# Halving the slot of the first expert layer: 23 slots of 256 rows become 39 slots of 128 rows

## What is computed

```
logits = x2 @ router_w
probs = softmax(logits); top_p, top_e = top_k(probs, 2)
for e in range(8):                                  # on the rows routed to e
    h = gelu(xd @ w_in[e] + b_in[e])                # 256 -> 256
    y = h @ w_out[e] + b_out[e]                     # 256 -> 256
out[token] += y * top_p
```

## Time and profile before

| what | value |
|---|---|
| runs | 763.7, 765.05 and 768.45 us, median 765.05 |
| profiled execution | 768.91 us, its span 767.2 us |
| mean granted clock of PE in it | 0.871 of full speed |
| busy share of the span | PE 75%, DVE 74%, POOL 57%, ACT 49% |
| the stage of the first mixture | about 303.8 to 410 us of the span |

### The profile page before, as it was taken

The page is one execution under the profiler, slowest core; times in us unless marked ns, Lnnn a source line. Parts: engine busy times, 40 slices in busy tenths (PEclk is TensorE's granted clock), DMA queues, the critical chain, the costliest instruction groups (busy, mean ns, idle before and its releaser), DMA issues.

```text
span 767.2 us, 17859 instructions
## 1 busy us (share of the span) xinstructions
PE 573.0 (75%) x6556; PEld 516.7 (67%) x6556; DVE 567.7 (74%) x1058; ACT 374.3 (49%) x567; POOL 434.3 (57%) x382
## 2 busy tenths in 40 slices
PE   5847889999999640698781556307999999999960
PEld 4636889889888530586671344206999999999950
DVE  3973579999998658587663677696777777778747
ACT  1754348777776540798560566622434343434320
POOL 7574468888898513764404885344455555555330
PEclk9988589999999885799987676657999999999995
DMA  8301001211221241699554232201011111112118
GB/s 280 99 4 29 28 2 36 71 51 55 70 68 41 73 142 54 191 309 278 151 169 144 82 99 75 80 3 56 31 55 44 56 44 54 46 51 49 36 56 309
DMA packets 35157, 68.50 MB, mean 89 GB/s; under 512 B 5761, under 2 KB 21890, under 8 KB 34818
## 3 DMA queue, kind: packets, MB, share of 16 engines
q1 hardware_dynamic: 25442, 42.70, 17.4%
q0 software_dynamic: 7488, 20.46, 9.4%
q10 hardware_dynamic: 2144, 4.19, 1.5%
HBM read 49.90 MB, written 17.43 MB: 88 GB/s over the span
## 4 chain that ended last, share of the span: by engine, by line
PE 46%; DVE 25%; issue 8%; ACT 7%; DMA 6%; POOL 6%; DVEq 1%; SPq 0%; ACTq 0%; POOLq 0%
PE banks L1249 43%; DMA sorted_y<-slot_region 2%; POOL wb_region L586 2%; PE banks L1448 2%; DVE x_res L1175 1%; DVE w_region L920 1%; DVE heads L912 1%; DVE w_region L925 1%; ACT w_region L692 1%; DMA w_region<-token_y 1%; DVE slot_region L1130 1%; DMA slot_region<-normed_rows,index 1%; DVE w_region L1060 1%; ACT w_region L625 1%; DVE slot_region L1060 1%
## 5 line engine op out<-in xcount | busy, mean ns | idle before, releaser
L1249 PE MATMUL banks<-w_region 128*128 128x128 f16 (+5 forms) x1948 | 175.7, 252 | 31.9 <-POOL w_region L548 12.1
L1249 PEld LDWEIGHTS banks<-w_region 128*128 128x128 f16 (+1 forms) x1948 | 161.0, 126 | 42.0 <-POOL w_region L548 12.4
L1249 PE MATMUL banks<-w_region,wb_region 128*128 (+1 forms) x1000 | 121.8, 278 | 11.3 <-DMA wb_region<-wk 6.7
L557 POOL DMA_INDIRECT slot_region<-normed_rows,index x85 | 94.8, 1115 | 51.0 <-PE banks L1448 21.7
L595 POOL DMA_INDIRECT token_y<-slot_region,lg x39 | 65.6, 1681 | 101.5 <-DVE slot_region L1130 101.2
L1249 PEld LDWEIGHTS banks<-w_region,wb_region 128*128 128x128 f16 (+1 forms) x1000 | 101.1, 106 | 22.9 <-issue 7.8
L759 ACT ACTIVATE wb_region<-wb_region 128x1024 f32<-128x1024 f32 x39 | 41.3, 1058 | 148.5 <-DVE wb_region L1115 148.5
L1249 PE MATMUL banks<-slot_region,staging 128*128 128x128 f16 x1872 | 112.9, 221 | 0.7 <-DVE staging L1106 0.7
L1249 PEld LDWEIGHTS banks<-slot_region,staging 128*128 128x128 f16 x1872 | 108.1, 99 | 1.0 <-issue 0.9
L1106 DVE COPY staging<-w_region 128x2048 f16 x78 | 54.5, 701 | 46.1 <-PE banks L1249 45.6
L1249 PE MATMUL banks<-wb_region,w_region 128*128 (+1 forms) x344 | 55.0, 311 | 23.2 <-DVE slot_region L1130 13.0
(11 more groups left out here) (237 smaller groups left out, 1126.1 us busy)
## 6 DMA issues: line engine op xcount, KB each, us to landing
staging<-w_t SPq DMA_DIRECT2D x24, 512.0 KB, 4.3
sorted_y<-slot_region SPq DMA_DIRECT2D x23, 256.0 KB, 5.6
w_region<-w_t SPq DMA_DIRECT2D x8, 512.0 KB, 5.5
x_res<-x SPq DMA_DIRECT2D x4, 512.0 KB, 9.4
staging<-w_in SPq DMA_DIRECT2D x4, 512.0 KB, 3.5
normed_rows<-w_region SPq DMA_DIRECT2D x16, 128.0 KB, 1.7
staging<-w_out SPq DMA_DIRECT2D x4, 512.0 KB, 3.7
normed_rows<-wb_region SPq DMA_DIRECT2D x16, 128.0 KB
```

The costliest lines, as they stand in the source:

```text
L557: g.indirect_dma_start(out=m.rows[:, j % m.RING, a, :], out_offset=None, in_=rows_dram, in_offset=bass.IndirectOffsetOnAxis(ap=index[:, q: ...
L1249: return t.matmul(o, a, b, start=start, stop=stop)
```

## The change

The first mixture gets slots of one tile as well: 39 slots of 128 rows. The ring of gathered rows holds 8 slots of 128 rows (before 3 of 256) and runs 5 slots ahead (before 2). The ring of outputs holds 6 of 128 rows (before 3 of 256). A chunk of weights is handled in every second round, 0 to 38, on SP, ACT and DVE. The scratch area of the routing grows by 100 words. The slot functions themselves are unchanged and read `m.A` and `m.SW`.

```
-    TILES = (2, 1)
+    TILES = (1, 1)
...
-            m.RING, m.AHEAD, m.YB = ((3, 2, 3), (8, 4, 4))[layer]
+            m.RING, m.AHEAD, m.YB = ((8, 5, 6), (8, 4, 4))[layer]
...
             for j in range(NSLOTS[0] + 4):
-                if RINGED.start + 2 + j < RINGED.stop:
-                    stage(RINGED.start + 2 + j)
-                elif 0 <= j - len(RINGED) < 4:
-                    stage(RINGED.stop + j - len(RINGED))
+                if j % 2 == 0 and RINGED.start + 2 + j // 2 < RINGED.stop:
+                    stage(RINGED.start + 2 + j // 2)
+                elif j % 2 == 0 and 0 <= j // 2 - len(RINGED) < 4:
+                    stage(RINGED.stop + j // 2 - len(RINGED))
                 if j >= 4:
                     keep_y(j - 4)
...
-                if PRE + A_CH + s in WITH_SLOTS:
-                    split_hi(PRE + A_CH + s)
+                if s % 2 == 0 and PRE + A_CH + s // 2 in WITH_SLOTS:
+                    split_hi(PRE + A_CH + s // 2)
...
-                    if PRE + A_CH + s in WITH_SLOTS:
-                        split_lo(PRE + A_CH + s)
+                    if s % 2 == 0 and PRE + A_CH + s // 2 in WITH_SLOTS:
+                        split_lo(PRE + A_CH + s // 2)
```

More of the change, by code:

```diff
@@ L129, in build @@
         cb_s, at = carve(W1R, at, [NB, D], F32)
-        route0, _ = carve(W1R, ln1.end, [1600], F32)
+        route0, _ = carve(W1R, ln1.end, [1700], F32)
         assert at <= 65536
```

## The result

The changed kernel takes 772.63 us (median of 4 runs, 772.4 to 773.16), the kernel before 766.67 (median of 4, 763.7 to 768.45). The ratio is 1.0095, 95% interval 1.0058 to 1.0133. In a later comparison of 7 runs with 22 it was 1.007 (1.0043 to 1.0097). The profiled executions are 772.51 us (span 770.8) and 768.91 (span 767.2).

A forecast was written before the change was run, and what follows sets the result against it. TensorE's sequencer was to bind slots of 128 rows at 2.46 us. The stage summed to 103.4 us, a gain of 0.3; routing and last store made it -0.9, 768.9 to 768.0, and 3.9 off gave 764 us, range 753 to 777.

The forecast's parts named there:

- a small further cost in each round: Rival: TensorE's value load, or a similar small cost per round, takes longer than summed; 766 to 775 us, chance 0.18.
- The mechanism: First mixture: TensorE's sequencer needs 2.46 us per slot, above ACT's 1.9 and DMA's 2.0, and becomes the period.
- issue does not bind: Rival: the sequencer's 0.127 us spacing is only pacing, rounds go by ACT and DMA at 2.0 us; 747 us, chance 0.14.
- 36 x 2.46: Rounds 3 to 38 of the first mixture, each 2.46 us of issue by TensorE's sequencer: 88.6 us.
- chunk 38's share: First mixture: the late load of chunk 38 delays ACT and stores behind it; 1.0 us taken, ends 0 and 4.
- my sum: First mixture's stage, first gather to end of last eviction: 103.4 us against 103.7 before, a gain of 0.3.
- The tail: End of the first mixture's stage, from issue of the last first layer to the last eviction: 4.8 us.
- The head: Stage start: first gather to first transposes 4.2 us, rounds 0 to 2 4.3 us, 0.5 added for PE's lower clock.
- the shift: Whole kernel: the median of the runs lies 3.9 us below the profiled execution, taking 768.0 to 764 us.
- that rival: TensorE's value load is longer than summed: 3 us at the median, 7 us if a quarter take 1.0; 767 to 771.
- The clock did not fall: Rival: idle gaps in each round lower PE's clock, a slot costs about 3.1 us; 775 to 787 us, chance 0.12.
- the routing: Outside the stage: comparing 1248 columns in place of 1472, with POOL's multiply and two comparisons, together -0.3 us.

The follow-up runs named there:

- Experiment 1: The changed kernel with TensorE reading expert 0's weights from fixed addresses in the first mixture, 12 address computations per slot gone: 764.33 us, ratio 0.9951 to the kernel before.
- Experiment 2: The changed kernel with a second, unused value load per slot in the first mixture: 804.55 us, ratio 1.0459 to the kernel before.
- Experiment 3: The kernel before (slots of 256 rows) with TensorE reading expert 0's weights from fixed addresses in the first mixture: 767.29 us, ratio 0.998.
- Experiment 5: The changed kernel with VectorE copying each slot's first-layer weights to a fixed place at the start of its round: 766.3 us, ratio 0.9997 to the kernel before.
- experiment 6: The changed kernel with SP loading chunk 38 once chunk 35, not 37, is split on the odd side: 772.8 us, ratio 1.0082 to the kernel before.
- experiment 7: The kernel before (slots of 256 rows) with SP's wait for chunk 38 eased, its load starting one round earlier: 758.9 us, ratio 0.9907.

## Why the prediction was wrong

The range of 753 to 777 held the 772.6 us, but it was that wide for rivals which did not come, and the forecast's own 759 to 769 missed. The direction was wrong: 764, a gain of 0.9 us, against a loss of 0.6 to 1.3%. The time fell where a small further cost in each round was foreseen, 766 to 775 at a chance of 0.18.

**The mechanism was right.** The waits for L1130 and for stores are gone, "issue" ends PE's waits, and rounds are of nearly equal length, paced by TensorE's sequencer. Experiments 1, 2 and 3 show it from three sides: take away its work and rounds shrink, add to it and they grow by no less than was added, take the same away under longer rounds and nothing moves that can be measured. Experiment 5 shows it with everything computed. The rival "issue does not bind" is refuted.

**The step that failed is the term "36 x 2.46".** A steady round is 2.58 us, and the mean of rounds 3 to 38, from the load at 312.65 to about 406.9, is 2.62: 94.3 us in place of 88.6, with chunk 38's share in it (1.0 in my sum). I built the round of its fastest pieces, each read where nothing paused. The whole round of before that I set beside it was 2.7, and I put the difference down to "a short pause" and left it out, as if it were an accident. Such pauses come in most rounds. On the mean of the 18 steady rounds the three semaphore instructions take 0.35 us where the sum has 0.30, the 12 address computations 1.56 where it has 1.52, and the value load with what follows it 0.67 where it has 0.64. What makes the pauses was not tried. The 0.12 us by which a steady round is longer is 4.3 us over 36 rounds, most of the 5.4 us by which the stage missed the sum (below).

**The tail** was 5.9 us (406.9 to 412.83), not 4.8. The head was 8.6 us (304.05 to 312.65) where the sum has 9.0. The three parts give 108.8 us against the 103.4 of the sum.

**The base was wrong too.** I took 3.9 us off, because the profiled execution of before lay that far above the median of the three runs shown. The changed kernel's profiled execution has no such excess: 772.51 against a median of 772.63. The sum with its measured terms and no shift is 768.9 - 0.9 + 5.4 = 773.4, and 772.5 was measured: outside the stage 1.5 us were saved where the sum has 0.6. So of the 8.5 us between forecast and result 5.4 are terms of the stage and 3.9 the shift, less these 0.9. The shift rested on three runs. The kernel before had a median of 766.67 with a fourth, and 768.95, 766.24 and 770.27 in the later sessions (19, 22 and 17 runs), so 765.05 was on the low side, and 768.9 is a usual time for it. A second reading, that the execution of before had lost time to its waits, stays open. Experiment 3's execution would fit it: it is 5.1 us shorter, with 2.3 us less of DVE's wait for stores, 4.7 less of PE's for L1130 and a stage 6.6 us shorter, but its addresses are fixed. The changed kernel's runs scatter less, 3.0 us in 7 runs against 8.1 in 22 of before beside them, but its profiled execution in that session lay 2.1 above its median.

**The other terms.** The value load's median in the stage is 0.304, so that rival did not happen. Six of the 39 loads last over 0.35 us, up to 0.74, which is part of the 2.62. The clock did not fall: 1.00 from 345 on, with gaps in each round. The micro-idles that make the clock oscillate by the Trainium skill (TensorE: Matmul & The Clock Gate, A second HAM failure mode), which it tells of a kernel with matmuls of 512 columns, find no counterpart in these rounds. Chunk 38 cost about what I gave it in the profile (the stage is 0.9 us shorter with its wait eased), and nothing that could be measured in the runs (experiment 6). From L1056 to the first gather the routing was 0.4 us shorter, where the sum has 0.3.

**Where the expected gain went.** The change removes 15% of the rows and the 13 us of waiting for L1130 in the trace of before, and pays 16 more rounds of issue. That this is the balance is argued, not measured piece by piece. The stall at chunk 38, on the other hand, did not need it: easing one wait on SP gives 0.9% with the large slots (experiment 7).

## What to carry to other kernels

Before a tile is halved, count what is issued per tile whatever its size, here 12 address computations and one value load, and measure a whole round of the sequencer with its pauses; that is the floor for the smaller tile. An engine that reads as 85% busy may be paced by its own sequencer: look for "issue" as what ends its waits, and for groups of matmuls that take longer than elsewhere at the same shape and clock (here 1.1 us against 0.84). When a stage's stretches slow down together, look for a wait that asks for more than it needs before changing the tiling.

## What the runs showed of the hardware that I had not expected

- A `FUSED_REGOPS` of 0.046 us takes 0.12 to 0.13 us of TensorE's sequencer, and a value load of 0.30 us some 0.65 with the register operation and assertion behind it. A second load per slot added 0.84 us to a round that the sequencer sets, since in every second round a load also lasted longer.
- The granted clock stayed at 1.00 for 65 us with TensorE's weight loads busy 60% of the time. Ahead of the transposes its matmuls paused 0.3 to 0.7 us in each round of 2.6.
